# The experts' second product moved behind the linear attention's piece and the value product

## The reference

```
h = tok(x)                        # windowed DFT, mel filters, log, DCT, projection
h = h + attn_topk(layernorm(h))   # A: 12 heads of 16; only the 100 largest scores of a row are kept
h = h + moe8(layernorm(h))        # B: 8 experts, 2 of them weighted; gate/up product, clipped gate, down product
h = h + performer(layernorm(h))   # C: linear attention with relu features (64 per head)
h = h + moe16(layernorm(h))       # D: 16 experts, 8 of them weighted; gelu between two products
```

## Time and profile before

| | |
|---|---|
| median of 3 runs | 2541.39 us (2525.52 to 2543.54) |
| profiled execution, its time | 2534.2 us |
| its span | 2532.1 us |
| mean granted clock | 0.893 |

### The profile page before, as it was taken

The page is one execution under the profiler, slowest core; times in us unless marked ns, Lnnn a source line. Parts: engine busy times, 40 slices in busy tenths (PEclk is TensorE's granted clock), DMA queues, the critical chain, the costliest instruction groups (busy, mean ns, idle before and its releaser), DMA issues.

```text
span 2532.1 us, 41098 instructions
## 1 busy us (share of the span) xinstructions
PE 2282.6 (90%) x11650; PEld 1893.2 (75%) x11650; DVE 1758.0 (69%) x6138; ACT 1582.5 (62%) x5065; POOL 2.6 (0%) x13
## 2 busy tenths in 40 slices
PE   5768888899999999999899998888997899999999
PEld 2446767677787877877778777777886788888887
DVE  2339888999988998899998998988642333333332
ACT  1289988888877888888788887864331322333221
POOL 0000000000000000000000000000000000000000
PEclk9975568888988999899899998988996899999999
DMA  3000002221111122122121221212332112111111
GB/s 71 0 1 1 1 20 53 55 53 49 49 44 47 54 51 52 45 53 54 44 53 48 52 55 41 55 45 58 90 94 75 66 72 72 71 58 49 71 72 42
DMA packets 160058, 128.80 MB, mean 51 GB/s; under 512 B 24018, under 2 KB 150904, under 8 KB 159480
## 3 DMA queue, kind: packets, MB, share of 16 engines
q1 hardware_dynamic: 157244, 123.02, 17.9%
q10 hardware_dynamic: 2592, 3.33, 0.4%
HBM read 122.80 MB, written 3.46 MB: 50 GB/s over the span
## 4 chain that ended last, share of the span: by engine, by line
PE 49%; DVE 31%; ACT 11%; issue 6%; another core or an unknown queue 2%; DMA 1%; DVEq 1%; SPq 0%; ACTq 0%
PE bank L527 13%; PE bank L887 10%; PE bank L867 10%; ACT late L1012 5%; PE bank L641 3%; DVE late L1495 3%; DVE late L1357 3%; DVE late L1472 3%; DVE late L1475 3%; DVE late L1469 3%; DVE late L1465 2%; DVE late L1629 2%; PE bank L763 2%; PE bank L606 2%
## 5 line engine op out<-in xcount | busy, mean ns | idle before, releaser
L1012 ACT ACTIVATE late<-arena,late 125x250 bf16<-125x250 f32 x1152 | 565.8, 500 | 1.4 <-DVE late L1343 1.2
L527 PE MATMUL bank<-extra,wgu 128*128 128x250 f32 x1536 | 434.8, 433 | 1.6 <-issue 1.5
L1731 DVE TENSOR_TENSOR pair<-pair,arena 128x500 f32<-128x500 f32 x192 | 130.3, 679 | 372.6 <-PE bank L887 315.7
L527 PEld LDWEIGHTS bank<-extra,wgu 128*128 128x128 f32 x1536 | 323.3, 220 | 44.9 <-issue 5.2
L1186 ACT ACTIVATE pair<-bank 128x500 f32<-128x500 f32 x192 | 104.0, 585 | 328.9 <-PE bank L867 321.5
L641 PEld LDWEIGHTS bank<-vaug,late 125*125 125x125 f32 x1536 | 229.0, 223 | 98.7 <-ACT late L1023 76.5
L867 PE MATMUL bank<-xT,late 128*128 128x250 f32 (+1 forms) x1536 | 280.8, 388 | 0.0
L887 PE MATMUL bank<-late,pair 128*125 128x192 f32 x1536 | 273.3, 331 | 0.0
L641 PE MATMUL bank<-vaug,late 125*125 125x17 f32 x1536 | 228.4, 284 | 49.0 <-ACT late L1023 47.8
L606 PE MATMUL bank<-late 16*125 16x251 f32 x768 | 253.6, 456 | 16.7 <-ACT arena L989 15.7
L887 PEld LDWEIGHTS bank<-late,pair 128*125 128x125 f32 x1536 | 246.6, 187 | 26.0 <-issue 25.4
(11 more groups left out here) (189 smaller groups left out, 3706.9 us busy)
## 6 DMA issues: line engine op xcount, KB each, us to landing
arena<-d_comb_rows SPq DMA_DIRECT2D x64, 500.0 KB, 6.2
wdn<-in_b_d SPq DMA_DIRECT2D x192, 96.0 KB, 1.9
late<-comb_rows SPq DMA_DIRECT2D x128, 125.0 KB, 3.1
wgu<-in_b_g SPq DMA_DIRECT2D x192, 64.0 KB
wgu<-in_b_u SPq DMA_DIRECT2D x192, 64.0 KB
late<-comb_rows SPq DMA_DIRECT2D x128, 62.5 KB, 2.6
wgu<-in_b_g SPq DMA_DIRECT2D x192, 32.0 KB
wgu<-in_b_u SPq DMA_DIRECT2D x192, 32.0 KB
```

Source lines behind the costliest of these rows:

```text
L527: ins = pe.matmul(dst, lhs(t), rhs(t), start=t == 0, stop=t == 1)
L1012: ins = sc.activation(mk[:, n_par(u), t, :] if k == 3 else junk[:, t, :], s_sb[:, ub, t, 0:N], ACT.Sign, bias=thr[:, (n_par(u) + k + 1) % ...
L1731: dv.tensor_tensor(hid[:, s % 2, :, :], gl[:, s % 2, :, :], c, ALU.mult).then_inc(hid_set[1], 1)
```

## The change

In TensorE's loop over the slots the call of `m0_down` moves from in front of the piece of C to behind `a_pv`, so that the order becomes: C's piece, value product, down product, the small pieces, first product. No instruction is added or removed, no semaphore changes, and the lists of VectorE, ScalarE, GpSimdE and SP stay as they are.

```diff
@@ -808,9 +808,6 @@
                 if b is not None:
                     ge(pe, v_set, min(b + 4, B))
                     comb_transpose(0, b, b % 2)
-                step = m0_at(T, DOWN_AT)
-                if step:
-                    m0_down(*step)
                 step = m0_at(T, CQ_AT)
                 if step:
                     b, t = step
@@ -828,6 +825,9 @@
                         project(1, b, bank[7], w["c_p"])
                 if was[0]:
                     a_pv(*was)
+                step = m0_at(T, DOWN_AT)
+                if step:
+                    m0_down(*step)
                 b = at_slot(T, LG_AT)
                 if b is not None:
                     route(0, b, b % 2)
```

## The result

| | before | changed |
|---|---|---|
| median, us (4 runs each) | 2542.47 | 2628.59 |
| lowest to highest | 2525.52 to 2547.3 | 2623.64 to 2639.24 |
| ratio, 95% interval | | 1.0357 [1.0297, 1.0416] |
| span, mean granted clock of the profiled execution | 2532.1, 0.893 | 2637.2, 0.862 |

The change makes the kernel 86 us slower: the forecast side, but more than twice the 39 us of the sum and above the range.

What follows compares the result with a forecast made beforehand. No engine alone was the bound, but a chain of waits through TensorE's first product into the tanh. Chain entries (32.2 us) and half clock (4.1 + 2.6) made 39 us: 2573 us, or 2580 against the median; range 2558 to 2610.

Steps and rivals of the forecast that it cites:

- the forecast side: Slower by over 1% (above 2567 us), the side of the forecast and the clock rival together; chance 0.80.
- the sum: All added costs of the later down product together: 39 us, between 28 and 46.
- The path: Chain through TensorE's slots, always leaving by the first product into the tanh; anything put before that product lengthens it.
- The count: Chain entries into TensorE, 385 to 1902 us: 43 of 50 pay 0.70 us for the down product, 30.1 us.
- The half-clock term: Dearer down products at half clock: 4.1 us at 7 early entries, 2.6 us at 9 entries of L754.
- The early stretch: 385 to 545 us, value product alone: all 10 chain entries pay, and the stretch takes about 10 us more.
- The wait for bank 6: VectorE's `add_experts` (L1257) behind the twelfth down product, once per batch: nothing likeliest, 16 us as upper end.
- The clock rival: TensorE's idle times merge and grow, so its clock falls more often: 26 us more, 2606 us; chance 0.2.
- No change: VectorE's own list sets the pace and TensorE's shifts fall into its slack: stays at 2541 us; chance 0.14.
- faster: C's piece and the value product fill TensorE's wait for the hidden units: 25 us saved, 2516 us; chance 0.06.

Runs made afterwards that it cites:

- f1: Kernel before, with extra matmuls that nobody reads behind the value product in all but the twelfth of a batch's slots; down product stays in front: 2570.31 us.
- f2: Changed kernel, with extra matmuls that nobody reads where the down product had been, in front of C's piece: 2579.36 us.
- e1: Changed kernel, with the bias product L698 left in front of C's piece and only the down product proper behind the value product: 2597.75 us.
- e4: Changed kernel, with the old order in the 17 slots before block C begins: 2614.64 us.
- h3: Kernel before, with extra matmuls that nobody reads in three waits of a batch (last L754, first `c_qk`, L763): 2495.97 us, ratio 0.9864.
- h1: Kernel before, with extra matmuls that nobody reads in two waits of a batch (last L754, first `c_qk`): 2553.37 us, ratio 1.0081.
- f5: Changed kernel, with extra matmuls that nobody reads in three waits of a batch (last L754, first `c_qk`, L763): 2564.47 us, ratio 1.0124.
- e2: Changed kernel, with the old order in two of a batch's twelve slots, those of the first `c_qk` and the last L754: 2611.7 us.
- f3: Changed kernel, with extra matmuls that nobody reads in two waits of a batch (last L754, first `c_qk`): 2608.42 us, ratio 1.0265.
- g1: Kernel before, with the value product ahead of the last L754 in that slot of each batch alone: 2530.22 us, ratio 0.9981.

## Why the prediction was wrong in size

- **The path.** Right in kind. Anything put between a wait of C or of the value product and the first product lengthens the time (f1); the waits before L705 went, those before L641, `c_qk` and the features came, and ScalarE's L1105 and VectorE's L1626 wait longer by 77 and 65 us. L754's idle time is 3.22 us, not 3.7: TensorE itself comes to it later than before.
- **The count: 43 entries at 0.70 us, 30.1 us (with the down product's own entries 32).** The 50 entries are there in the trace, and the growth of idle time, 36 us, is of that size. But the reasoning was too simple: it held the old chain fixed, and the chain moved into TensorE, with 74 entries and 114 down products on it. No run isolates this term from the clock. The upper end of 46 us had no working.
- **The half-clock term, 4.1 + 2.6 = 6.7 us. This step failed.** By the account it is 60 us in the profiled pair (some 35 us by the estimate for the middle executions), and f2 gets 38 to 50 us back by keeping TensorE occupied. I had priced the down product at the clock of the slot it moves into, and taken the clock itself as given. The change took 0.7 us of work out of the stretch in front of each wait, and with that the clock fell more often.
- **The forgotten product.** L698 moves with L705 into the worst slot of a batch. The diff showed one call, the order showed L698 in the early slot, and I left it out. e1 puts 31 us on it, more than the 22 us that the product had on the chain; the account has 29 of the 35 us between the profiled executions as half clock, so what it costs and what it does to the clock can't be parted.
- **The early stretch: 10 us.** From the first first product to the 21st it took 23 us more by the trace; e4 gives 14 us back, in overlapping intervals.
- **The wait for bank 6, nothing to 16 us.** In the window of the waits above VectorE waits 1.1 us in all before L1257, in 2 waits. It was rightly put at nothing.
- **The clock rival (2606 us, 0.2).** The right mechanism, at 26 us for 60 (some 35 in the middle executions). It counted falls at fixed places, 9 `c_qk` slots and half of the seven L745 slots in which the clock had stayed full, while in the runs the falls changed places. The per-batch distance grew by 6.4 us (105.8 to 112.2, where I had 1.4 to 2.5), of which 2.5 in the `c_qk` slot and 2.3 in that of L754. The test that I named for it, a mean clock off 0.91 by more than 0.01, came out at 0.87. The rule of the Trainium skill cited there ("TensorE: Matmul & The Clock Gate", "What's actually happening": the throttled state is the default, activity releases it) agrees with f2 and h3, where added activity raised the clock from 0.87 to 0.95 and from 0.91 to 0.98. It does not foresee h1, where 49 us of added work left it at 0.91.
- **"No change" and "faster".** Both fell. VectorE did not take up the shift: its busy time fell by 50 of 960 us. The wait for the hidden units went, as the faster case had it, but the value product itself now waits longer than before (32.5 us for 12.4 in the window of the waits above).

What stays open: why the clock falls in one slot and not in another that idles as long, and how much of the 86 us the order would cost with the clock held. With the three waits filled in both orders the difference is still 66 us by the ratios (f5 less h3); of the 67 us between the two profiled executions the account has 41 as half clock, 17 as idle time, 9 as work. So f5 and h3 do not hold the clock alike, and that difference is no measure of the order alone.

## What to carry to other kernels

Before moving a piece of work out from in front of a wait, ask what it did there besides its result: on a TensorE that is 90% busy it also kept the clock up, and leaving it out there cost 38 to 50 us (f2 against the changed kernel) though it is less work. Read the clock slot by slot, and after any fix look at the next wait, because the fall can move there, as in e2, f3, h1 and g1; filling two waits of three lost 20 us, filling the third as well gained 55. And when a call moves, price everything that the call issues.

## What the runs showed of the hardware

- Work that nobody needs can make a kernel faster: 86 us more of it on TensorE, 35 to 42 us less time (h3), with the clock of 545 to 1505 us at 0.98 for 0.91 in the profiled executions. Where to put it decides: with two waits filled it cost 20 us (h1).
- The same idle time of 1.7 us ahead of the same product dropped the clock in one kernel (3.67 us for `c_qk`) and not in another (1.93 us, e1): an idle time alone does not tell whether the clock falls behind it.
